# Layer 0 of a four-layer cross-attention kernel: two token buffers in turn, and the output weights loaded in the middle of the attention

## What is computed

```
h    = concat([ctx, x])                      # 461 tokens per batch, 512 features
q    = x @ q_w + q_b                         # 16 heads of 32
k, v = split(h @ kv_w + kv_b)
attn = softmax(mask(q k^T / 32)) @ v
out  = rmsnorm(attn @ out_w + out_b + x)
x    = gelu(out @ mlp_w1 + mlp_b1) @ mlp_w2 + mlp_b2 + x
```

## Time and profile before

| what | us |
|---|---|
| median of 3 runs | 3515.48 |
| lowest, highest | 3509.28, 3518.54 |
| the profiled execution's own time | 3518.28 |
| its span in the profile | 3516.5 |
| TensorE busy in the span | 3100.3 (88%) |
| mean granted clock of TensorE | 0.932 of full speed |

### The profile page before, as it was taken

One profiled execution on the slowest core, in us unless ns is written; L12 is line 12 of the kernel. 1 busy time (PEld: TensorE's weight loads), 2 busy tenths in 40 slices (PEclk: granted clock), 3 DMA queues, 4 the chain that ended last, 5 costly groups with the idle time before them and its releaser, 6 DMA issues. The chain is left out here.

```text
span 3516.5 us, 47941 instructions
## 1 busy us (share of the span) xinstructions
PE 3100.3 (88%) x17313; PEld 2580.9 (73%) x17313; DVE 1927.5 (55%) x3923; ACT 1472.9 (42%) x3391; POOL 863.5 (25%) x879
## 2 busy tenths in 40 slices
PE   4899779796877889999999988999999988969996
PEld 3677469454544489988999888998989878945662
DVE  2445342517874276666566666657566654247773
ACT  1444342211011144456544554446444444237770
POOL 0222310213541231123011431104011140055622
PEclk9999789898988899999999999999999998979986
DMA  3222020100001140014201241102301123021201
GB/s 109 62 64 67 18 96 1 59 0 3 0 12 36 44 129 26 27 49 131 66 27 44 65 145 42 52 19 83 119 30 48 34 67 96 13 75 53 65 3 38
DMA packets 140413, 186.04 MB, mean 53 GB/s; under 512 B 26191, under 2 KB 107996, under 8 KB 140188
## 3 DMA queue, kind: packets, MB, share of 16 engines
q1 hardware_dynamic: 127460, 147.24, 13.7%
q0 software_dynamic: 12544, 35.77, 3.3%
q10 hardware_dynamic: 184, 0.05, 0.0%
HBM read 165.88 MB, written 13.86 MB: 51 GB/s over the span
## 5 line engine op out<-in xcount | busy, mean ns | idle before, releaser
L63 PE MATMUL l2a<-l_arena,l_arena 128*128 128x400 f32 (+2 forms) x1856 | 652.8, 352 | 38.4 <-DVE l_arena L2648 13.6
L65 PE MATMUL l2a<-l_arena,l_arena 128*128 128x400 f32 (+2 forms) x1856 | 633.4, 341 | 0.0
L64 PE MATMUL l2a<-l_arena,l_arena 128*128 128x400 f32 (+2 forms) x1856 | 632.9, 341 | 0.0
L63 PEld LDWEIGHTS l2a<-l_arena,l_arena 128*128 128x128 f32 (+1 forms) x1856 | 353.3, 190 | 61.0 <-issue 49.9
L64 PEld LDWEIGHTS l2a<-l_arena,l_arena 128*128 128x128 f32 (+1 forms) x1856 | 354.5, 191 | 2.7
L65 PEld LDWEIGHTS l2a<-l_arena,l_arena 128*128 128x128 f32 (+1 forms) x1856 | 352.8, 190 | 2.0
L2513 ACT ACTIVATE l_arena<-l2a 121x384 fp32r<-121x384 f32 (+1 forms) x208 | 99.6, 479 | 442.8 <-PE l2a L2288 442.8
L2308 PE MATMUL l2a<-l_arena,l_arena 121*128 121x384 f32 (+1 forms) x768 | 279.4, 364 | 3.2 <-DVE l_arena L2714 3.2
L2310 PE MATMUL l2a<-l_arena,l_arena 121*128 121x384 f32 (+1 forms) x768 | 263.9, 344 | 0.0
L2309 PE MATMUL l2a<-l_arena,l_arena 121*128 121x384 f32 (+1 forms) x768 | 263.2, 343 | 0.0
L2163 POOL DMA_DIRECT2D p_dram_layer<-l_arena x128 | 62.7, 495 | 726.0 <-DVE l_arena L2714 724.3
(11 more groups left out here) (417 smaller groups left out, 6913.8 us busy)
## 6 DMA issues: line engine op xcount, KB each, us to landing
l_arena<-in_L_xattn_wq_dram SPq DMA_DIRECT2D x32, 512.0 KB, 3.5
l_arena<-in_L_xattn_wk_dram SPq DMA_DIRECT2D x32, 512.0 KB, 4.5
l_arena<-in_L_xattn_wv_dram SPq DMA_DIRECT2D x32, 512.0 KB, 3.6
l_arena<-in_L_xattn_wo_dram SPq DMA_DIRECT2D x64, 256.0 KB, 2.6
l_arena<-ctxT_hi POOLq DMA_DIRECT2D x16, 724.0 KB, 4.6
l_arena<-ctxT_lo POOLq DMA_DIRECT2D x16, 724.0 KB, 6.1
l0mlp_staged<-in_L_xattn_mlp_w_dram SPq DMA_DIRECT2D x16, 512.0 KB, 4.2
l2mlp_staged<-in_L_xattn_w_fc_dram SPq DMA_DIRECT2D x16, 512.0 KB, 4.2
```

What stands on the lines that cost most here:

```text
L63: pe.matmul(out, cut_a(a.hi), cut_b(b.hi), start=start, stop=False)
L64: pe.matmul(out, cut_a(a.hi), cut_b(b.lo), start=False, stop=False)
L65: return pe.matmul(out, cut_a(a.lo), cut_b(b.hi), start=False, stop=stop)
```

## The change

1. `hcat` becomes two buffers with a semaphore each, used by even and odd batches. Batch 1's tokens are loaded at the end of `setup`; in the attention SP loads the tokens of b+2 right after batch b's `rest_done`.
2. SP's loop has a new order: wait for `rest_done`, tokens of b+2, store `ctxT`, mask of b+1. `X` moves from b = 0 to b = 3.
3. The two `kv_w` buffers become halves of one tensor `k.out_w`. At b = 4, SP loads `out_w` into it, and `out_b` and `mlp_b2` into buffers of their own. The output block loads nothing.
4. The first mask is loaded ahead of `v_bias`; POOL clears two padding tiles in `setup` instead of one.

```diff
@@ setup @@
+    k.hcat = [pre.enter_context(nc.sbuf_tensor(f"hcat{i}", [T0, NT0, D], F32)) for i in range(2)]
+    k.out_w = pre.enter_context(nc.sbuf_tensor("kv_then_out_w", [P, KT, D], F32))
+    k.kv_w = [k.out_w[:, 2 * i:2 * i + 2, :].rearrange("p k n -> p (k n)") for i in range(2)]
...
-            pool.memset(k.hcat[:, 3, :], 0.0).then_inc(hcat_padded, 1)
+            for i in range(2):
+                pool.memset(k.hcat[i][:, 3, :], 0.0).then_inc(hcat_padded, 1)
...
             sp.wait_ge(zeroed, 1)
             load_params(sp, (1, 2))
+            sp.wait_ge(hcat_padded, 2)
+            load_tokens_of(sp, k, ins, 1)
@@ layer0_attention, SP @@
             def load_tokens(b):
-                sp.wait_ge(tokens_turned, KT * b)
-                load_first_tokens(sp, k, ins, b)
+                sp.wait_ge(tokens_turned, KT * (b - 1))
+                load_tokens_of(sp, k, ins, b)
...
+            load_mask(0)
             sp.dma_start(v_bias[:], ins["L0_xattn_kv_b"].partition_broadcast(P)).then_inc(weights_loaded, 16)
-            load_mask(0)
             for b in range(B):
-                if b + 1 < B:
-                    load_tokens(b + 1)
-                    load_mask(b + 1)
-                if b == 0:
-                    sp.dma_start(k.X[:], ins["x"].rearrange("b l d -> l b d")).then_inc(x_loaded, 16)
                 sp.wait_ge(rest_done, KT * (b + 1))
+                if b + 2 < B:
+                    load_tokens(b + 2)
                 for part, src in (("hi", hT[b % 2].hi), ("lo", hT[b % 2].lo)):
                     sp.dma_start(k.ctxT[part][b].bitcast(F32), src[:, :, 0:S + 1].bitcast(F32)).then_inc(ctxT_stored[b % 2], 16)
+                if b + 1 < B:
+                    load_mask(b + 1)
+                if b == 3:
+                    sp.dma_start(k.X[:], ins["x"].rearrange("b l d -> l b d")).then_inc(x_loaded, 16)
+                if b == 4:
+                    sp.wait_ge(w_split, 2 * KT)
+                    load_features(sp, k.out_w, ins["L0_xattn_out_w"], k.out_loaded)
...
@@ layer0_attention, PE @@
-                    pe.wait_ge(tokens_loaded, 48 * (b + 1))
+                    pe.wait_ge(tokens_loaded[b % 2], 48 * (b // 2 + 1))
@@ layer0_output @@
         @block.sync
         def _(sp):
-            load_features(sp, out_w, ins["L0_xattn_out_w"], loaded)
-            sp.dma_start(out_b[:], ins["L0_xattn_out_b"].partition_broadcast(L)).then_inc(loaded, 16)
-            sp.dma_start(mlp_b2[:], ins["L0_xattn_mlp_b2"].partition_broadcast(L)).then_inc(loaded, 16)
+            prefetch(sp)
...
-            pe.wait_ge(loaded, 48)
+            pe.wait_ge(k.out_loaded, 48)
```

More of the change, by code:

```diff
@@ L134, in setup @@
     k.states = ctx.enter_context(nc.sbuf_tensor("states", [P, KT, 2, B], F32))
-    k.hcat = pre.enter_context(nc.sbuf_tensor("hcat", [T0, NT0, D], F32))
-    k.kv_w = [pre.enter_context(nc.sbuf_tensor(f"kv_w{i}", [P, 2 * D], F32)) for i in range(2)]
-    k.tokens_loaded = nc.alloc_semaphore("l0_tokens_loaded")
+    k.hcat = [pre.enter_context(nc.sbuf_tensor(f"hcat{i}", [T0, NT0, D], F32)) for i in range(2)]
+    k.out_w = pre.enter_context(nc.sbuf_tensor("kv_then_out_w", [P, KT, D], F32))
+    k.kv_w = [k.out_w[:, 2 * i:2 * i + 2, :].rearrange("p k n -> p (k n)") for i in range(2)]
+    k.out_rows = {n: pre.enter_context(nc.sbuf_tensor(f"{n}_row", [L, D], F32)) for n in ("out_b", "mlp_b2")}
+    k.out_loaded = nc.alloc_semaphore("l0_out_loaded")
+    k.tokens_loaded = [nc.alloc_semaphore(f"l0_tokens_loaded{i}") for i in range(2)]
     k.kv_loaded = [nc.alloc_semaphore(f"l0_kv_loaded{t}") for t in range(KT)]
@@ L203, in _ @@
             sp.wait_ge(hcat_padded, 1)
-            load_first_tokens(sp, k, ins, 0)
+            load_tokens_of(sp, k, ins, 0)
             for t in range(2):
-                sp.dma_start(k.kv_w[t][:], ins["L0_xattn_kv_w"][t * P:(t + 1) * P, :]).then_inc(k.kv_loaded[t], 16)
+                sp.dma_start(k.kv_w[t], ins["L0_xattn_kv_w"][t * P:(t + 1) * P, :]).then_inc(k.kv_loaded[t], 16)
             for r in range(2):
@@ L226, in _, with load_tokens_of @@
             last.then_inc(turned, 1)
-def load_first_tokens(sp, k, ins, b):
+def load_tokens_of(sp, k, ins, b):
     whole = 3 * T0
     rest = S - whole
[L233 to L237, removed]
+    context, hcat = ins["ctx_2048"], k.hcat[b % 2]
+    sp.dma_start(hcat[:, 0:3, :], context[b, 0:whole, :].rearrange("(t p) d -> p t d", p=T0)
+                 ).then_inc(k.tokens_loaded[b % 2], 16)
+    sp.dma_start(hcat[0:rest, 3, :], context[b, whole:S, :]).then_inc(k.tokens_loaded[b % 2], 16)
+    sp.dma_start(hcat[rest:rest + L, 3, :], ins["x"][b]).then_inc(k.tokens_loaded[b % 2], 16)
 def layer0_attention(nc, k, ins, ctx, attT):
@@ L372, in _ @@
                 sp.wait_ge(w_split, 2 * (t - 1))
-                sp.dma_start(kv_w[t % 2][:], ins["L0_xattn_kv_w"][t * P:(t + 1) * P, :]).then_inc(kv_loaded[t], 16)
+                sp.dma_start(kv_w[t % 2], ins["L0_xattn_kv_w"][t * P:(t + 1) * P, :]).then_inc(kv_loaded[t], 16)
+            load_mask(0)
             sp.dma_start(v_bias[:], ins["L0_xattn_kv_b"].partition_broadcast(P)).then_inc(weights_loaded, 16)
-            load_mask(0)
             for b in range(B):
-                if b + 1 < B:
-                    load_tokens(b + 1)
-                    load_mask(b + 1)
-                if b == 0:
-                    sp.dma_start(k.X[:], ins["x"].rearrange("b l d -> l b d")).then_inc(x_loaded, 16)
                 sp.wait_ge(rest_done, KT * (b + 1))
+                if b + 2 < B:
+                    load_tokens(b + 2)
                 for part, src in (("hi", hT[b % 2].hi), ("lo", hT[b % 2].lo)):
                     sp.dma_start(k.ctxT[part][b].bitcast(F32), src[:, :, 0:S + 1].bitcast(F32)).then_inc(ctxT_stored[b % 2], 16)
+                if b + 1 < B:
[5 more added lines that the diff above has]
+                    load_features(sp, k.out_w, ins["L0_xattn_out_w"], k.out_loaded)
+                    sp.dma_start(k.out_rows["out_b"][:], ins["L0_xattn_out_b"].partition_broadcast(L)
+                                 ).then_inc(k.out_loaded, 16)
+                    sp.dma_start(k.out_rows["mlp_b2"][:], ins["L0_xattn_mlp_b2"].partition_broadcast(L)
+                                 ).then_inc(k.out_loaded, 16)
             for s in range(2):
@@ L387, in _ @@
             sp.wait_ge(x_loaded, 16)
+            sp.wait_ge(k.out_loaded, 48)
         @block.gpsimd
@@ L407, in unit @@
                 if kind == "t":
-                    pe.wait_ge(tokens_loaded, 48 * (b + 1))
+                    pe.wait_ge(tokens_loaded[b % 2], 48 * (b // 2 + 1))
                     for i in range(NT0):
-                        mm = pe.transpose(out[:, i * T0:(i + 1) * T0], hcat[:, i, j * P:(j + 1) * P],
+                        mm = pe.transpose(out[:, i * T0:(i + 1) * T0], hcat[b % 2][:, i, j * P:(j + 1) * P],
                                           k.ident[0:T0, 0:T0])
@@ L1041, in _, with layer0_output @@
                 add(b)
-def layer0_output(nc, k, ins, ctx, attT, split):
+def layer0_output(nc, k, ins, ctx, attT, split, prefetch):
     with ExitStack() as own:
@@ L1050, in sb @@
             return own.enter_context(nc.sbuf_tensor(name, shape, F32))
-        out_w = sb("out_w", [P, KT, D])
-        out_b = sb("out_b", [L, D])
-        mlp_b2 = sb("mlp_b2", [L, D])
+        out_w, out_b, mlp_b2 = k.out_w, k.out_rows["out_b"], k.out_rows["mlp_b2"]
         Y = sb("Y", [L, B, D])
@@ L1062, in layer0_output @@
                       [("out", B, "d"), ("hT", 2 * KT, "ad")])
-        loaded = k.sems.take("l0o_loaded")
         residual = k.sems.take("l0o_residual")
@@ L1086, in _ @@
             k.sems.clear_ended(pool)
-            pool.wait_ge(loaded, 48)
+            pool.wait_ge(k.out_loaded, 48)
             for b in range(B):
@@ L3370, in program @@
                 hT = Split(own, nc, "l0_hT", [P, KT, B * L], side="right")
-                layer0_output(nc, k, ins, ctx, attT, hT)
+                layer0_output(nc, k, ins, ctx, attT, hT, lambda sp: None)
             mlp(nc, k, ctx, "l0mlp", hT, ins["L0_xattn_mlp_w1"], ins["L0_xattn_mlp_w2"], "L0_xattn_mlp_b1",
```

## The result

| | us |
|---|---|
| changed kernel, median of 4 runs (lowest, highest) | 3477.32 (3473.24, 3485.75) |
| kernel before, median of 4 runs beside it | 3517.01 (3509.28, 3518.57) |
| ratio | 0.9895, 95% interval 0.9869 to 0.9921 |
| the profiled execution's own time, and its span | 3481.11, 3479.3 |

It is faster. The span fell by 3516.5 - 3479.3 = 37.2 us where I had 30.9.

What follows compares the result with a forecast made beforehand. TensorE, busy 88% of the span, was held by waits on batch 2's tokens and the output block's loads; -20.98 - 2.90 - 7.53 + 0.5 = -30.9 us from the 3515.48 median gave 3484.6 us, range 3476 to 3494.

Steps and rivals of the forecast that it cites:

- The wait on batch 2's tokens, -20.98: Layer 0 attention: TensorE's wait on the DMA into hcat before batch 2's transposes goes whole, -20.98 us.
- the half clock behind it, -2.9: Attention, batch 2's transposes to head 8's scores: the half clock after the idle wait goes, -2.9 us.
- The output block, -7.5: Layer 0 output block: TensorE starts with the block instead of waiting for its loads, -7.5 us.
- The start, +0.5 between 0 and 2: Kernel start: batch 1's early token load delays kv_w's third piece, +0.5 us, between 0 and 2.
- The clock of the output block: Output block: clock may rise up to 3 us earlier, worth 1.5 us at most; counted as nothing.
- shifts as a whole: Everything behind layer 0's output block is released by it and shifts as a whole.
- Number 1: Rival at the start: early token load holds up parameters or kv_w, up to 9.3 us, 3493.4 us; 10 in 100.
- Numbers 2 and 3: Only the output block gains, 3508.5 us, 3 in 100; token loads late each batch, 3540.4 us, 1 in 100.
- Number 4: Rival: the output wait goes to POOL or the clock, block gives only half, 3488 us; 6 in 100.
- The rule of the largest divisor: Token DMAs: engine count is the largest up to 16 dividing the slowest dimensions, so 116 partitions get 4.

Runs made afterwards that it cites:

- second pair: Second profiles of the two kernels, from the runs before_again (kernel before) and again (changed kernel); the two spans differ by 26.0 us.
- before_again: The kernel before run against itself, no edit: ratio 0.9993, median 3508.75 us of 12 runs.
- x_late: The kernel before with X loaded at b = 3 instead of b = 0: ratio 0.9998 to the kernel before.
- late1: The changed kernel with batch 1's token load moved from the end of setup to behind v_bias: ratio 0.9924 to the kernel before.
- x_early: The changed kernel with X loaded at b = 0 again: ratio 0.9925 to the kernel before.
- again: The changed kernel run again, no edit: median 3481.82 us against 3509.45, ratio 0.9926 to the kernel before.
- split112: The changed kernel with each token load's first DMA cut into partitions 0 to 111 and 112 to 115: ratio 0.9896 to the kernel before.
- late1_split112: The changed kernel with both edits, of late1 and of split112: ratio 0.9898 to the kernel before.

## Why the prediction was right or wrong

- **The wait on batch 2's tokens, -20.98, and the half clock behind it, -2.9.** Right. From the first scores to batch 2's transposes it was 28.32 us and is 7.18: -21.1; the stretch after it fell by 2.84. In the second pair these are -20.0 and -1.95, because in `before_again` the clock was back at 99 instead of 102. Nothing was late next, as argued. The cause that I named, `X` and the stores ahead of the tokens, was right in part: without `X` there, 11.8 us of the wait stayed (`x_late`).
- **The output block, -7.5.** Right: -7.48 and -7.3 in the two pairs. POOL's clears were hidden as I said: DVE takes the first sum at 409.84, 3.5 us after it is ready.
- **The start, +0.5 between 0 and 2.** The size failed: +3.15 and +1.9 at the first scores, the first outside my bounds. ACT took the third piece at 35.00 and 34.38, where I had 31 to 33, and the q projection started at 38.64 and 38.01, where I had 35.6 to 37.6. I had the mechanism (`q_w` and `kv_w` have shares on the four engines), but counted on part of the lateness being absorbed, and took the engines as free from 27 on. The third piece came 4.1 and 3.7 us later in the two pairs. In the windows of the changed kernel the DMA engines (last two numbers) were busy for all of the time from 26 to 30:

```profile
26.00:28.00 2.00, 0.36 (x2) 0.00 (x1) 1.47 (x3) 2.00 (x5) 0.00 (x0) 1.00 1.02 230
28.00:30.00 2.00, 1.03 (x4) 0.67 (x4) 2.00 (x4) 1.34 (x4) 0.00 (x0) 1.00 1.06 241
```

They moved 230 and 241 GB/s; before the change it was 371 in the first, and in `late1`, with the token load out of the way, 335 and 328. Fully busy engines moved less beside the tokens, and the prediction's +0.5 had no row for that.
- **The clock of the output block, counted at nothing with a gain of up to 1.5 us.** In the two pairs the block took 1.5 and 0.9 us longer, because the clock rose 6 us after TensorE's start in it, where it had risen after 3.1 and 4.4 us in the two profiles of the kernel before. I had bounded one side only. But a cost of the change is not shown: `x_early`, whose attention ends where that of `again` does (400.33 against 400.27) and whose block starts without a wait too, has the clock rise 3.5 us after TensorE's start, and the block takes 53.28 us against 53.02 and 53.68 before:

```profile
404.00:405.00 1.00, 1.00 (x2) 0.28 (x2) 0.00 (x0) 0.00 (x0) 1.00 (x2) 0.66 0.03 8
```

Over the twelve profiles the rise came 2.9 to 4.5 us after the start where the wait stood (five profiles) and 2.9 to 6.2 us where it was gone (seven). That too differs between executions.
- **Layers 1 to 3, "shifts as a whole".** True only within some 10 us per execution. Summed over layer 0, -24.9 and -27.0 us were gained, not 30.9. The measured 39.7 us between the first medians were more than layer 0's gain; that the surplus is a favourable draw of clock spells is argued from the profiles and not measured for the medians. The later ratio, 0.9926, is 26 us (20 to 32). So the mechanism was right and the sum some 4 to 6 us too large, and the first measurement missed it on the other side.
- **The rivals.** Number 1 was the direction of the error, at 2 to 3 us of its 9.3: the parameters were not held up (21.84 against 21.52), `kv_w` was. Numbers 2 and 3 did not occur: TensorE never waited on `hcat` in the attention of the two profiles. Number 4 did not either: with its clock counted in, the block gave 6.0 and 6.4 us, not half of 7.5. The rule of the largest divisor, that I took from the Trainium skill (DMA: Bandwidth & Descriptors, "Why a DMA increments its semaphore by 16 and not by 1"), agrees with `split112`: 16 divides 112, and the share while batch 1's tokens load is 0.96, where 116 partitions had 0.26.

The fastest version is `split112` (3475.23) or `late1_split112` (3470.38), against 3481.82 for the changed kernel on the same chip; between the two the runs do not decide, and their intervals just touch that of the changed kernel (0.9909 to 0.9942).

## What to carry to other kernels

Before a prefetch is moved ahead of something, look at the share of DMA engines that it uses, and not only at its bytes: here a token load of 9 us on a quarter of the engines made a weight piece land 4 us later, and another held TensorE's start back by about 4 us. Give a double buffer the credit for a wait only after asking what else stood in that queue: here `X` was 8 to 9 of some 20 us, and the mask and the stores stood ahead of the tokens as well. And where an engine's clock changes by itself, take the gain from the stages that the change touches, in two profiles of each kernel; one pair of spans held 12 us from layers that were not changed.

## What the runs showed of the hardware that was not expected

- The granted clock differs between executions of one program: layer 3 took 442.2 and 450.9 us in two profiles of the changed kernel, and one stretch of 10 us ran at 1.00 in the first and at 0.50 in the second.
- The tokens on 116 partitions moved at 0.26 of the engines and about 100 GB/s; cut into 112 and 4, TensorE's first instruction came 3.6 to 4.6 us earlier.
